# Flamingo block with routed experts: the early tile list in twelve parts, index and weight loads elsewhere on SyncE, placings in three tiles of four, and batch 2's projections sooner

## The reference

```python
x = x + tanh(g_xattn) * attention(layernorm(x), ctx, ctx)        # 16 heads, projections Wq, Wk, Wv, Wo
xf = layernorm(x)                                                # 3584 rows
w, e = top_k(softmax(xf @ w_router.T), 2)
y = (silu(xf @ w1[e]) * (xf @ w3[e])) @ w2[e]                    # hidden width 352
x = x + tanh(g_ffn) * sum(w * y)
```

## Time and profile before

| | us |
|---|---|
| median of 3 runs | 906.64 (906.26 to 909.02) |
| the profiled execution's own time | 914.7 |
| its span in the trace | 912.8 |
| TensorE (PE) busy | 868.9 (95% of the span) |
| VectorE (DVE) busy | 495.1 (54%) |
| ScalarE (ACT) busy | 423.0 (46%) |
| GpSimd (POOL) busy | 475.3 (52%) |
| granted TensorE clock, mean of the span | 0.979 |

### The profile page before, as it was taken

One profiled execution on the slowest core, in us unless ns is written; L12 is line 12 of the kernel. 1 busy time (PEld: TensorE's weight loads), 2 busy tenths in 40 slices (PEclk: granted clock), 3 DMA queues, 4 the chain that ended last, 5 costly groups with the idle time before them and its releaser, 6 DMA issues.

```text
span 912.8 us, 21112 instructions
## 1 busy us (share of the span) xinstructions
PE 868.9 (95%) x7209; PEld 689.5 (76%) x7209; DVE 495.1 (54%) x1161; ACT 423.0 (46%) x1086; POOL 475.3 (52%) x565
## 2 busy tenths in 40 slices
PE   7799999999999999999998999889998999999995
PEld 6578888888888888888877888766776777777773
DVE  3456666866775875776687786562541222222221
ACT  2246556565655565556554565454422222222221
POOL 6244443454455445545544455344677565656652
PEclk9899999999999999999999999988999999999998
DMA  6756666777768667557654566425434343443432
GB/s 159 156 142 168 165 168 158 172 168 185 170 157 198 144 139 165 135 124 170 138 136 110 130 153 138 94 77 186 65 59 59 59 68 60 65 69 59 62 61 29
DMA packets 99631, 112.27 MB, mean 123 GB/s; under 512 B 28860, under 2 KB 80820, under 8 KB 99528
## 3 DMA queue, kind: packets, MB, share of 16 engines
q1 hardware_dynamic: 79144, 92.33, 43.0%
q0 software_dynamic: 18240, 16.83, 11.9%
q10 hardware_dynamic: 2144, 1.77, 0.9%
HBM read 35.48 MB, written 17.53 MB: 58 GB/s over the span
## 4 chain that ended last, share of the span: by engine, by line
PE 83%; DMA 6%; DVE 3%; issue 3%; another core or an unknown queue 1%; ACT 1%; POOL 1%; ACTq 1%; POOLq 0%; DVEq 0%
PE ps L1267 16%; PE ps L1044 11%; PE ps L1050 9%; PE ps L1015 9%; PE ps L1327 9%; PE ps L1029 9%; PE ps L1055 7%; DMA stack<-negmax_t 5%; PE ps L1192 3%; PE ps L1151 2%; PE ps L1286 2%; DVE negmax L785 2%; PE ps L1231 1%; PE ps L1070 1%
## 5 line engine op out<-in xcount | busy, mean ns | idle before, releaser
L785 DVE TENSOR_REDUCE negmax<-ps 112x2 f32<-112x750 f32 x256 | 240.5, 939 | 160.4 <-PE ps L1044 155.9
L523 ACT ACTIVATE probs<-ps 125x448 f32<-125x448 f32 x384 | 208.4, 543 | 238.5 <-PE ps L1015 224.7
L1015 PE MATMUL ps<-stack 97*125 97x224 f32 x768 | 194.2, 336 | 6.8 <-DMA stack<-negmax_t 6.3
L356 POOL DMA_DIRECT2D stack<-negmax_t x128 | 69.4, 544 | 241.2 <-ACT negmax_t L581 232.6
L1015 PEld LDWEIGHTS ps<-stack 97*125 97x125 f32 x768 | 131.8, 191 | 32.5 <-DMA stack<-negmax_t 9.1
L1044 PE MATMUL ps<-stack 96*112 96x376 f32 x512 | 143.6, 361 | 8.0 <-DVE negmax L785 7.7
L446 POOL DMA_INDIRECT out_dram<-y,idx x63 | 100.5, 1595 | 78.5 <-PE ps L1231 23.4
L623 ACT ACTIVATE silu<-ps 128x352 f32<-128x352 f32 x63 | 29.2, 463 | 187.0 <-PE ps L1267 171.7
L971 DVE TENSOR_TENSOR h<-silu,ps 128x352 f32<-128x352 f32 x63 | 32.8, 520 | 145.0 <-PE ps L1267 127.7
L1050 PE MATMUL ps<-wv_sb,ctx_t 128*125 128x256 f32 x384 | 102.4, 390 | 0.2 <-DVE bo_gated L836 0.2
L1029 PE MATMUL ps<-probs,v_sb 125*32 125x112 f32 x3072 | 101.3, 265 | 0.0
(11 more groups left out here) (204 smaller groups left out, 1212.5 us busy)
## 6 DMA issues: line engine op xcount, KB each, us to landing
stack<-split SPq DMA_DIRECT2D x252, 150.0 KB
ctx_t<-in_ctx_dram SPq DMA_DIRECT2D x32, 375.0 KB, 4.7
stack<-split SPq DMA_DIRECT2D x126, 94.0 KB
stack<-split SPq DMA_DIRECT2D x126, 56.0 KB
out_dram<-xa SPq DMA_DIRECT2D x32, 112.0 KB, 4.3
xn_scratch<-xn SPq DMA_DIRECT2D x32, 112.0 KB, 3.8
xa<-in_x_dram SPq DMA_DIRECT2D x7, 448.0 KB, 5.7
w_sb<-in_L_ffn_w_dram SPq DMA_DIRECT2D x8, 352.0 KB
```

The lines of the kernel that those rows point to most:

```text
L356: gp.dma_start(dst[:, :, SKP + SQ * h:SKP + SQ * h + SQ], negmax_t[4 * h:4 * h + 4, half, :].bitcast(f32)).then_inc(s_nmrow[half][c % NSLO ...
L523: act.activation(probs[:, g % 2, ch, :], ps[0:KW, EXPB + k % 2, 0:4 * SQ], ACT.Exp).then_inc(s_exp, 1)
L785: dve.tensor_reduce(negmax[:, half, :, p4], ps[0:SQ, m1:m2 + 1, 0:SK], axis=AX.X, op=ALU.max, negate=True).then_inc(s_max, 1)
L1015: last = pe.matmul(ps[0:KW, EXPB + k % 2, QW * m:QW * m + QW], stack[:, place_of(b), p, KW * ch:KW * ch + KW], stack[:, place_of(b), p, SK ...
```

## The change

- **Early tile list.** early_map has twelve parts, at k = 2, 5 and 8 of steps 24, 25, 28 and 29. owners, shifted and behind are cut into compared, scaled and added; the running sum of summed becomes four calls of partial.
- **SyncE.** The index loads (now seven: NI is 7) move from the end of step 28 to the head of step 30. In step 31 w3_hi and w2's first part are issued ahead of both stores. Batch 0's stack loads: SyncE issues ten, six of them before klo is ready.
- **GpSimd.** Its stack_first issues the other six, at the end of step -3. The sixteen placings of the tile stage come in three tiles of four, up to turn 21. queries is a function now and is called for batch 2 in step -2.
- **ScalarE** issues no stack loads.
- **TensorE.** third_batch projects keys and queries of batch 2 behind step -2 (with like functions on ScalarE, VectorE and GpSimd), and step -1 has no projections of a batch. Batch 0's maxima alternate between two pairs of banks, so VectorE may be one behind. The output bias moves into step -1 (k = 5 to 9), the turned maxima of batch 0 to k = 6 of step -1 and behind it. VectorE makes xn of the first three batches in slots 0 and 1 of steps -3 and -2.

```diff
-    NI = 8
+    NI = 7
...
+        MAP_STEPS = [GB * SNAP + n for n in (8, 9, 12, 13)]
...
         def max_banks(c, t):
+            if c == 0 and t % 2:
+                return EXPB, EXPB + 1
             return (BB_, BC) if c == B - 1 and t in (3, 5) else (MAXB, MAXB + 1)
+
+        def stacked(n):
+            return 256 * (n // NSLOT + 1) - (96 if n % NSLOT == 0 else 0)
 
...
+                if i == LAST - 2:
+                    sp.wait_ge(s_map, 1)
+                    for g in range(2):
+                        sp.wait_ge(s_scat[g], placed(SNAP + 1, g))
+                    sp.sem_inc(s_met_sp, 1)
+                    for t in range(NI):
+                        load_idx(t)
+                if i == LAST - 1:
+                    sp.wait_ge(s_exp_ps, 12 * (B - 2))
+                    sp.sem_inc(s_met_sp, 1)
+                    sp.wait_ge(s_stack[(B - 1) % NSLOT], stacked(B - 1))
+                    sp.wait_ge(s_nmrow[0][(B - 1) % NSLOT], 32 * ((B - 1) // NSLOT + 1))
+                    sp.dma_start(w3_hi[:, :, :], w3[:, P:2 * P, :].rearrange("e p f -> p e f")).then_inc(s_w13, 16)
+                    load_w2(0)
...
+                    if s == 0:
+                        sp.wait_ge(s_qlo, 1)
+                        sp.wait_ge(s_khi, DC)
+                        for g in range(3):
+                            from_high(g)
+                        sp.wait_ge(s_klo, DC)
+                        for g in range(2):
+                            from_low(g)
+                    else:
+                        wait(sp, s_klo, DC * (s + 1))
+                        sp.sem_inc(s_met_sp, 1)
+                        wait(sp, s_qlo, s + 1)
+                        for g in range(4):
+                            from_high(g)
+                            from_low(g)
                 if a is not None and NSLOT - 1 <= a < B - 1:
...
+            def stack_first():
+                src, dst = split[:, 0, :, :].bitcast(f32), stack[:, place_of(0), :, :].bitcast(f32)
+                gp.wait_ge(s_qlo, 1)
+                gp.wait_ge(s_khi, DC)
+                rows, pr = slice(96, 128), slice(3 * DC, 4 * DC)
+                gp.dma_start(dst[0:32, pr, 0:SKP], src[rows, :, KHI:KHI + SKP]).then_inc(s_stack_gp, 16)
+                gp.dma_start(dst[0:32, pr, SKP:KQ], src[rows, :, QHI:QHI + QW]).then_inc(s_stack_gp, 16)
+                gp.dma_start(dst[64:96, pr, :], src[rows, :, KHI:KHI + KQ]).then_inc(s_stack_gp, 16)
+                gp.wait_ge(s_klo, DC)
+                gp.dma_start(dst[32:64, pr, :], src[rows, :, KLO:KLO + KQ]).then_inc(s_stack_gp, 16)
+                rows, pr = slice(64, 96), slice(2 * DC, 3 * DC)
+                gp.dma_start(dst[32:64, pr, :], src[rows, :, KLO:KLO + KQ]).then_inc(s_stack_gp, 16)
+                gp.dma_start(dst[64:96, pr, :], src[rows, :, KHI:KHI + KQ]).then_inc(s_stack_gp, 16)
+
...
+                if i == -2:
+                    queries(2)
...
+                if i == FIRST:
+                    stack_first()
...
-                if 0 <= t - 1 < 2 * GB * TOP:
-                    place(NU - 2 + (t - 1) // (GB * TOP), (t - 1) % (GB * TOP) // TOP, (t - 1) % TOP)
+                n = t - 1 - t // 4
+                if t % 4 < 3 and 0 <= n < 2 * GB * TOP:
+                    place(NU - 2 + n // (GB * TOP), n % (GB * TOP) // TOP, n % TOP)
...
-                if i == -3:
-                    stack_first((2, 3))
                 if i == -2:
-                    act.wait_ge(s_wr_ps, 1)
-                    act.activation(wr_t[:, :, :], ps[:, 0, 0:DC * NE], ACT.Copy).then_inc(s_wr_t, 1)
+                    third_batch()
+                if i == -1:
+                    negmax_out(0, 1, PVB)
...
+            def partial(src, part):
+                old, new = (ct_a, ct_b) if part % 2 else (ct_b, ct_a)
+                if part == 0:
+                    link(dve.tensor_copy(ct_a[:, :], src[:, :]))
+                else:
+                    d = 1 << part - 1
                     dve.tensor_copy(new[:, 0:d], old[:, 0:d])
                     link(dve.tensor_tensor(new[:, d:NE], old[:, d:NE], old[:, 0:NE - d], ALU.add))
-                    old, new, d = new, old, 2 * d
-                return old
...
+            def compared(ends, n, at):
+                link(dve.tensor_tensor(e_cmp[:, 0:n, :], over_t(ends, n), at[:, 0:n].rearrange("p (t o) -> p t o", o=1).broadcast_to([1, n, NE]), ALU.is_le))
...
+            def scaled(out, factors, n):
+                link(dve.tensor_tensor(out[:, 0:n, :], e_cmp[:, 0:n, :], over_t(factors, n), ALU.mult))
+
+            def added(out, parts, n):
+                link(dve.tensor_reduce(out[:, 0:n], parts[:, 0:n, :], axis=AX.X, op=ALU.add))
 
...
                 n = EARLY
                 if part == 0:
                     link(dve.tensor_reduce(n_tiles[:, :], n_cmp[:, :, :], axis=AX.X, op=ALU.add))
-                    full = summed(n_tiles)
-                    link(dve.tensor_scalar(taken_c[:, :], full[:, :], float(EARLY), None, ALU.min))
-                if part == 1:
+                if part in (1, 2):
+                    partial(n_tiles, 2 * part - 2)
+                    partial(n_tiles, 2 * part - 1)
+                if part == 3:
+                    link(dve.tensor_scalar(taken_c[:, :], ct_b[:, :], float(EARLY), None, ALU.min))
                     dve.memset(taken[:, NE:NE + 1], 0.0)
+                if part == 4:
                     dve.tensor_copy(taken[:, 0:1], taken_c[:, 0:1])
                     link(dve.tensor_tensor(taken[:, 1:NE], taken_c[:, 1:NE], taken_c[:, 0:NE - 1], ALU.subtract))
                     link(dve.tensor_scalar(n_gap[:, :], taken[:, 0:NE], -1.0, float(PER_E), ALU.mult, ALU.add))
-                if part == 2:
-                    owners(taken_c[:, :], n, tile_no)
-                if part == 3:
-                    shifted(n_gap[:, :], n)
-                if part == 4:
-                    behind(taken[:, 0:NE], n)
                 if part == 5:
+                    compared(taken_c[:, :], n, tile_no)
+                if part == 6:
+                    added(e_tile, e_cmp, n)
                     dve.tensor_copy(e_idx[:, 0:n], e_tile[:, 0:n])
+                if part == 7:
+                    scaled(e_mul, n_gap[:, :], n)
+                if part == 8:
+                    added(s_tile, e_mul, n)
+                if part == 9:
+                    scaled(e_mul2, taken[:, 0:NE], n)
                     link(dve.tensor_tensor(s_tile[:, 0:n], s_tile[:, 0:n], tile_no[:, 0:n], ALU.add))
+                if part == 10:
+                    added(w_tile, e_mul2, n)
+                    dve.tensor_copy(s_idx[:, 0:n], s_tile[:, 0:n])
+                if part == 11:
                     link(dve.tensor_scalar(w_tile[:, 0:n], w_tile[:, 0:n], 1.0, None, ALU.max))
-                    dve.tensor_copy(s_idx[:, 0:n], s_tile[:, 0:n])
                     dve.tensor_copy(w_idx[:, 0:n], w_tile[:, 0:n]).then_inc(s_map, 1)
 
...
+                if k == 0 and b == 0:
+                    pe.wait_ge(s_max, 8)
...
-                    wait(pe, s_max, 8 * c + t)
+                    wait(pe, s_max, 8 * c + t - (1 if c == 0 else 0))
...
+            def third_batch():
+                pe.wait_ge(s_klo, 2 * DC)
+                pe.wait_ge(s_xn, 3)
+                for m in range(DC):
+                    last = pe.transpose(ps[:, BB_, P + SQ * m:P + SQ * m + SQ], xn[:, P * m:P * m + P], ident[0:SQ, 0:SQ])
+                last.then_inc(s_xn_ps, 1)
+                pe.wait_ge(s_v, KC)
+                pe.wait_ge(s_ctx[2], 16)
+                key_proj(2, 0, BC)
+                pe.wait_ge(s_xn_t, 3)
+                for m in range(DC):
+                    for n in range(DC):
+                        last = pe.matmul(ps[:, BB_, SQ * m:SQ * m + SQ], wq_sb[:, n, P * m:P * m + P], xn_t[:, n, :],
+                                         start=(n == 0), stop=(n == DC - 1))
+                last.then_inc(s_q_ps, 1)
+                pe.wait_ge(s_q_raw, 3)
+                key_proj(2, 1, BB_)
...
             for i in range(FIRST, LAST):
+                step(i)
+                if i == -2:
+                    third_batch()
                 if i == -1:
-                    pe.wait_ge(s_wr_t, 1)
-                step(i)
+                    negmax_turn(0, 1, PVB)
```

More of the change, by code:

```diff
@@ L531, in step @@
                         value_out(s, 0, BA)
-                    if k == 2 and b is not None:
+                    if k == 2 and b is not None and b > 0:
                         if a is not None:
@@ L754, in step @@
                 for k in range(12):
-                    if k == 0 and a is not None:
+                    if i <= FIRST + 1 and k in (0, 1) and 2 * (i - FIRST) + k < 3:
+                        n = 2 * (i - FIRST) + k
+                        wait(dve, s_xn_ps, n)
+                        dve.tensor_scalar(xn[:, :], xrow(n), mv1[:, 0, n, 0:1], rstd1[:, 0, n:n + 1], ALU.subtract, ALU.mult).then_inc(s_xn, 1)
```

(18 more changed lines are left out.)

181 lines of the change are left out of this document (87 added, 94 removed).

## The result

| | median, us | ratio to the kernel before | 95% interval |
|---|---|---|---|
| before, beside it | 907.83 (4 runs) | | |
| after | 921.52 (4 runs, 921.41 to 924.70) | 1.015 | 1.0104 to 1.0196 |

The prediction was 898.7 us with a range of 892.5 to 907, and 0.78 for faster. It was wrong in sign. On the median of the kernel before that was given first, 906.64, the measured ratio stands for 920 us. The profiled execution took 924.7 us, its span 923.0, against 914.7 and 912.8.

What follows compares the result with a forecast made beforehand. The prediction took TensorE, 83% of the span, as the bound, an edit being worth what it takes from TensorE's waits. Terms -3.0 - 6.0 + 0 + 0 + 1.0 = -8.0 us gave 898.7 us from 906.64, range 892.5 to 907.

Steps and rivals of the forecast that it cites:

- Seven index buffers: Tile stage, one index buffer fewer: +1 us taken, bounds 0 and +14.
- 4.7 + x + 1.5: Tile stage: time two turns hold with seven buffers, from addition to index issue, landing, and the addition's place behind the gather.
- x: Index load's landing time after issue, read as 1.3 to 2.8 us; from 2.2 the ring sets the pace.
- the slack of 8 us: Tile stage: gather's lead over TensorE's use, less some 2.5 us of transfer, to be used up before lateness costs.
- the ring: Rival, chance 0.13: the index ring sets the tiles' pace, +7 to +14 us in place of +1, 905 to 912.
- The start: Batch 0's and 1's first maxima: ScalarE's wait and TensorE's idle time won, -6.0 us, bounds -7.4 and -3.
- The early list: Step 24: the early tile list's stall goes when its instructions are spread, -3.0 us, bounds -3.8 and -1.5.
- The placings: Sixteen placings in three tiles of four, ending in turn 21: 0 us, bounds -4.0 and +1.
- The rival's reason: Placings rival, chance 0.13: the 4.0 us lost among the placings were GpSimd's lag, and go: 894.7 us.
- The weight loads: Step 31: two weight loads leave ahead of two stores, 0 us taken, bounds 0 and -1.5.
- the index loads' move: Index loads go to step 30, batch 31's stack loads come up to 5 us sooner: 0 taken.
- the sum on record: Whole kernel: the terms -3.0 - 6.0 + 0 + 0 + 1.0 = -8.0 us.

Runs made afterwards that it cites:

- eight buffers: The changed kernel with eight index buffers for seven, nothing else: 895.67 us, ratio 0.9849, tile stage 261.7 us.
- seven in the kernel before: The kernel before with seven index buffers for eight, nothing else: 927.45 us, ratio 1.0191, tile stage 284.4 us.
- three tiles ahead: The changed kernel, still seven index buffers, GpSimd gathering three tiles ahead instead of four: 895.60 us, ratio 0.9854.
- the addition first: The changed kernel, seven index buffers, the gather behind the addition in each of GpSimd's turns instead of in front: 896.62 us, ratio 0.9854.
- six buffers: The changed kernel with six index buffers for seven, still gathering four tiles ahead: 1161.7 us in one run.
- the nine traces of the old form: Traces of kernels with the early list in six parts; step 24 takes 19.74 to 22.54 us, against 17.39 to 17.50 in the new form.
- the start alone: The kernel before with only the change's start (ScalarE issues no stack loads, batch 2's projections sooner, two bank pairs), eight index buffers: 900.64 us, ratio 0.9899.

## Why the prediction was wrong

**Seven index buffers: the failed term.** Its mechanism is the one on record, and five runs bear it out: eight buffers, seven in the kernel before, three tiles ahead, the addition first (which repeats it) and six buffers. Its size was wrong: +1 us was taken, with +14 as the bound, and 28.6 us of stage were measured. Four things were wrong with "4.7 + x + 1.5" and what was made of it.

First, the 1.5 had no room for GpSimd's own 0.77 us between the landing of the index load and the gather, which the chain shows; so the circle closes at x = 8.43 - 4.83 - 0.77 - 1.29 = 1.5 us, not 2.2. x was read as 1.3 to 2.8, and the chain's seven index loads from 740 to 900 us have 1.69 to 2.68. The likeliest x already lay beyond the closing point.

Second, a turn with a placing is longer by 0.94 and a gap of 0.30, and the formula was only used for turns without.

Third, everything lands later among the placings: the chain's eight index loads from 640 to 740 us take 1.93 to 3.20 us, and its additions 3.84 to 4.97, not 3.87. With 2.5 for x two turns there need 4.83 + 2.5 + 0.77 + 1.29 + 1.24 = 10.6 us, an estimate of 1.1 us a tile over 4.21, and more with the longer additions. The trace has 1.3:

```profile
633.46 0.48 DVE L1067 TENSOR_SCALAR y<-ps,idx 128x256 f32<-128x256 f32 x1
634.76 1.59 POOL L495 DMA_INDIRECT out_dram<-y,idx  x1 [0.57 <-SPq L340]
...
659.01 0.48 DVE L1067 TENSOR_SCALAR y<-ps,idx 128x256 f32<-128x256 f32 x1
668.28 1.62 POOL L495 DMA_INDIRECT out_dram<-y,idx  x1 [0.30 <-issue]
```

The addition of tile 2 begins 1.30 us behind its y, that of tile 8 begins 9.27 us behind. So the slack of 8 us is gone in six turns, and the y of tile 12 is the first that comes late (5.92 us behind that of tile 11). The gather's transfer, which that slack took as 2.5 us, has 2.73 to 4.30 in the chain. From there on TensorE pays: tiles 16 to 25 take 49.3 us for 37.9 with eight buffers, 1.3 us more each; from tile 25 to 62, with the placings over, it is 164.8 for 154.0, 0.3 each.

Fourth, the chances: the ring was called a rival with 0.13, though the same text put its closing point in the middle of the values read for x. Its price was low too: a turn of 4.5 is 0.29 over 4.21, not 0.26, so 58 turns are 17 us, not 15. The Trainium skill's rule weighed there ("DMA: Bandwidth & Descriptors", section "SWDGE vs HWDGE vs iDMA"), that both engines' queues are served in turn by the same DMA engines, pointed the right way: no landing in the chains is at the short end of 1.3, and most are longer among the placings. That this serving in turn is the reason, no run shows.

**The start: right in kind, mis-sized.** 6.0 us predicted, 7.9 by the trace. Batch 1's query projection began at 21.36 in place of 26.00, batch 0's maxima ran from 32.49 to 41.43 (8.9 us, as worked out), and batch 1's first maximum came at 42.80, where 44.7 stood in the prediction. The loads of batch 1, taken as late next, were issued from 27.60 and were in nobody's way. Two things I had not seen. One is TensorE's clock: in the kernel before TensorE was busy 1.66 us from 20 to 26 and was granted 0.59 from 26 to 32, so that the query projection took 2.05 us; after, it was busy 5.57 us from 20 to 26 and was granted 1.00 throughout. The other is that the parts don't add: each of two of them, undone alone, takes back the whole.

```profile
20.28 0.36 ACT L594 ACTIVATE xn_t<-ps 128x224 f32<-128x224 f32 x1 [0.47 <-PE ps L1212]
...
21.36 1.04 PE L1238 MATMUL ps<-xn_t,wq_sb 128*128 128x112 f32 x8
...
32.49 3.47 DVE L845 TENSOR_REDUCE negmax<-ps 112x2 f32<-112x750 f32 x4
...
40.50 0.93 DVE L845 TENSOR_REDUCE negmax<-ps 112x2 f32<-112x750 f32 x1
...
42.80 0.93 DVE L845 TENSOR_REDUCE negmax<-ps 112x2 f32<-112x750 f32 x1
...
27.60 0.59 SPq L282 DMA_DIRECT2D stack<-split  x1
```

**The early list: right.** -3.0 predicted; against the nine traces of the old form step 24 gives 2.3 us (four of them), 3.6 (four, the first among them) and 5.0 (one). By time alone the gain is inside the intervals. The long small instruction did not vanish: one of 1.11 us stands at 486.88 now, ahead of the maximum of 488.02, which begins 3.12 us behind its forerunner. The step's length shows that less of it reaches TensorE there. The Trainium skill ("SBUF — State Buffer", section "Who interferes with whom") says that a VectorE instruction with two inputs in SBUF contends with a GpSimd instruction that reads SBUF; the trace agrees as far as this one tensor_tensor beside one of GpSimd's from 486.81 to 487.96 can. The instructions did stay exposed, as the prediction had it by that section; the price was 0.7 us beside the 2.42 of an undisturbed pair, not the 1.5 that I set against the term.

**The placings: the rival's number, not its reason.** I took 0 and gave 0.13 to the loss going away; in nine of nine traces it is gone, 5.4 us. The rival's reason was GpSimd's lag. A turn with a placing is indeed longer than I had it (4.47 us in the timelines, as from the addition at 647.42 to that at 651.89, not 4.35), but in the start alone that lag reached the 6.23 us above and TensorE didn't wait, so the slack of 8 us held there as the prediction said. In the kernel before the additions never begin more than 3.7 us behind their y, and of the 61 us from 650 to 711 the chain puts 12.1 down to "another core or an unknown queue" in the first trace and none in the second. What TensorE waits for there the traces don't name, and no run tells.

**The weight loads: right,** nothing by the run. They left at 593.89, 29.1 us ahead of the first y, where it had been 25.3 (609.92 to 635.23). For the index loads' move the 0 stands untested.

Without the ring the sum on record would have been -9.0; the eight-buffer kernel is 1.5% faster than before, 13.7 us on 906.64. By the traces its last y is 16.7 us sooner, and 5.8 of these are won in the tiles, counted at 0. How much of that is in the 13.7 isn't known, since on the same chip the placings alone gained nothing by time.

## What to carry to other kernels

A ring of buffers is passed on by a queue, so count its slack in turns of that queue, from the instruction that frees a buffer to the one that refills it, with every piece between (the first transfer, the other engine's issue, landing, and the waiting engine's own start), and do so for the longest turn and for landings as the busiest stretch has them. When one buffer less is wanted, shorten the look-ahead by one as well: that gave all 3% back here. To write the freeing instruction ahead of the waiting one in each turn is the same order under another name, as the two runs showed. And where a mechanism's deciding point lies inside the values that the trace shows for it, it is not a rival but half of the forecast.

## What the runs showed of the hardware

The first microseconds react with more than their waits. Repeated waits of 1.03 us, with TensorE busy 2.30 of 6 us, were followed by 12 us at half its clock (0.50 granted from 38 to 50 us), and together these made one missing bank pair worth 7.6 us.

Passing work from one engine to another is not free either: from the end of an addition's transfer to the issue of the index load on SyncE 1.0 us passes (743.55 to 744.51), and from that load's landing to GpSimd's gather another 0.77. And the same small transfer can take nearly twice as long in another stretch: in one execution the index loads of the chain landed in 1.93 to 3.20 us among the placings and in 1.69 to 2.68 behind them.
